# Cross stage of a decoder layer: values by head group, x2 turned behind the values, scores ahead of the slot scores, and the softmax division on VectorE

## The chip, the cores and the metric

One core of one Trainium2 chip. The metric is the device time of one execution in microseconds, as a median of runs. The engines are named as the profile names them: PE is TensorE's matmul, PEld its weight load, DVE VectorE, ACT ScalarE, POOL GpSimd, SP SyncE, which here issues the DMAs.

## The reference, cut to what matters

One decoder layer on x of 2 x 2048 tokens with 512 features, all float32: a Mamba-like mixer, a cross attention on a context of 77 tokens, and a feed-forward part in which 16 slots gather the tokens, 16 experts work on the slots, and the tokens read the slots back. The change touches the cross attention and the gathering of the slots:

```python
    def _L0_xattn_ref(x, context, q_w, q_b, k_w, k_b, v_w, v_b, o_w, o_b):
        ...
        q = (x @ q_w + q_b).reshape(B, T, H, D).transpose(0, 2, 1, 3)
        k = (context @ k_w + k_b).reshape(B, S, H, D).transpose(0, 2, 1, 3)
        v = (context @ v_w + v_b).reshape(B, S, H, D).transpose(0, 2, 1, 3)
        att = jnp.einsum('bhtd,bhsd->bhts', q, k) / jnp.sqrt(jnp.float32(D))
        causal = jnp.tril(jnp.ones((T, S), dtype=bool))
        att = jnp.where(causal[None, None, :, :], att, -jnp.inf)
        att = jax.nn.softmax(att, axis=-1)
        y = jnp.einsum('bhts,bhsd->bhtd', att, v)
        y = y.transpose(0, 2, 1, 3).reshape(B, T, C)
        return y @ o_w + o_b
    ...
    x = _layernorm(x + _L0_attn_ref(...), axis=-1)        # x1
    x = _layernorm(x + _L0_xattn_ref(x, ctx_1024, ...), axis=-1)        # x2
    x = _layernorm(x + _L0_ffn_ref(x, ...), axis=-1)
```

There are 16 heads of 32 features. The feed-forward part begins with an attention of the 16 slots over all tokens of x2, which the kernel computes with a running maximum and a running sum while it makes x2.

## The kernel before

The kernel runs five stages one after the other: tables, mixer, cross, experts, combine, each a block with its own programs for PE, ACT, DVE, POOL and SP, which meet only through semaphores. The cross stage (`cross_stage`) takes the 4096 tokens in 32 tiles of 128, 16 for each of two sequences. For tile t:

- `turn_x1` (PE, L934) turns x1 of the tile, `take_x1T` (ACT, L1017) copies it from PSUM, `queries` (PE, L943) multiplies it with the query weights, `take_queries` (DVE, L1080) adds the bias.
- `score` (PE, L954) makes the scores of the 16 heads with 77 context tokens. `take_scores` (DVE) adds the causal mask in the first tile of a sequence only (L1069), takes the maximum over the context (L1072) and subtracts it (L1074).
- `exponents` (ACT, L1021), `denominators` (DVE, sum L1102, reciprocal L1105), `normalise` (L1138) multiplies the 128 x 1232 exponentials with the reciprocals, in place.
- `turn_probs` (PE, L961) turns the probabilities into the four PSUM banks that held the scores, `take_probsT` (ACT, L1044) copies them out bank by bank, `weigh_values` (PE, L970) multiplies with the values, `take_yT` (ACT, L1060) copies the result, `project_out` (PE, L978) projects.
- `residual` (DVE, L1124) adds x1 plus bias, which `add_bias` (POOL, L1134) has made, and `norm` (DVE, L578 to L595, fifteen small instructions) makes the factors of the layernorm; `scale_rows` (ACT, L1050) writes x2.
- `turn_x2` (PE, L985), `take_x2T` (ACT, L1027), `slot_scores` (PE, L993), `slot_maxima` (DVE, L1089 to L1098), `slot_exponents` (ACT, L1033, L1036), `slot_sums` (DVE, L1110, L1112), `turn_slots` (PE, L1001), `take_slotsT` (ACT, L1055), `weigh_tokens` (PE, L1011) and `add_tokens` (DVE, L1118) carry the tile's x2 into the slots.

The order is written out by hand: each engine has a function `step` for one tile, in which stages of several tiles stand beside each other. The softmax of tile t + 1, the slot scores of tile t - 1 and add_tokens of tile t - 2 run in the step of tile t. `tiles` runs the steps 0 to 3, 14 to 17 and 30 and 31 written out, and 4 to 13 and 18 to 29 in hardware loops of two steps a turn. An engine takes its instructions in order, so one that waits holds up all behind it. `wait_later` leaves a wait out in the first tiles. PSUM: four banks `SC` for scores and turned probabilities, one each for `AV` (queries, then weighed values), `TO` (turned x2, projection, tokens' product), `SLOT` and `TOK` (turned x1, tokens' product). `add_tokens` must have read TOK and TO before x1 or x2 is turned into them.

SP loads x1 two tiles ahead and stores x2 and its transpose. In steps 1, 14 and 16 it fetches the first two, four and six of the 96 weight units of the experts into a ring of six.

The step of PE before:

```python
                def step(t, u, half, seq):
                    turn_probs(pe, t)
                    if before(t, 1):
                        turn_x2(pe, t - 1, 1 - u)
                    if ahead(t, 2):
                        turn_x1(pe, t + 2, u, half + 1)
                    weigh_values(pe, t, seq(0))
```

Of the kernel before, what the change touches and what calls it, by code (L numbers as in the profile page):

```python
# [876 lines left out]
def cross_stage(nc, io, hold, ring, ring_in):  # L877
    with Stage(nc, "crs") as st:
# [34 lines left out]
        HEAD_AT = [(h % HG) * GROUPS + h // HG for h in range(HEADS)]  # L913
# [43 lines left out]
        def turn_probs(pe, t):  # L957
            pe.wait_ge(s["normed"], t + 1)
            for i in range(HG):
                for h in range(GROUPS):  # L960
                    last = nc.tensor.transpose(SC[0:CTX, i, h * P:(h + 1) * P], pr[:, i * GROUPS + h, :], hold["ident"][:])  # L961
                last.then_inc(s["pr_turned"], 1)

        def weigh_values(pe, t, b):
            pe.wait_ge(s["prT_done"], HG * t + HG)

            pe.wait_ge(s["qT_done"], min(t + 2, TILES) if isinstance(t, int) else t + 2)
            for h in range(HEADS):
                g, r = h // HG, (h % HG) * HD
                last = nc.tensor.matmul(AV[r:r + HD, g * P:(g + 1) * P], hold["v"][:, b, h * HD:(h + 1) * HD], prT[:, HEAD_AT[h], :],  # L970
                                        start=True, stop=True)
            last.then_inc(s["av_done"], 1)
# [67 lines left out]
        def take_probsT(act, t):  # L1040
            wait_later(act, s["av_done"], t)
            for i in range(HG):
                act.wait_ge(s["pr_turned"], HG * t + i + 1)
                nc.scalar.activation(prT[:, i * GROUPS:(i + 1) * GROUPS, :].rearrange("p h t -> p (h t)"), SC[0:CTX, i, :], ACT.Copy).then_inc(s["prT_done"], 1)  # L1044
# [91 lines left out]
        def normalise(pool, t):  # L1136
            pool.wait_ge(s["rden_done"], t + 1)
            nc.gpsimd.tensor_tensor(pr[:], pr[:], broadcast(rden[:].unsqueeze(2), [P, HEADS, CTX]), ALU.mult).then_inc(s["normed"], 1)  # L1138
# [24 lines left out]
        with nc.Block() as block:  # L1163
# [26 lines left out]
            def _(pe):  # L1190
# [8 lines left out]
                def step(t, u, half, seq):  # L1199
                    turn_probs(pe, t)  # L1200
                    if before(t, 1):
                        turn_x2(pe, t - 1, 1 - u)
# [3 lines left out]
                    if before(t, 1):  # L1206
                        slot_scores(pe, t - 1, 1 - u)
                    if ahead(t, 1):
                        score(pe, t + 1, seq(1))
                    project_out(pe, t)  # L1210
# [13 lines left out]
            def _(act):  # L1224
# [4 lines left out]
                def step(t, u, half, seq):  # L1229
                    take_probsT(act, t)  # L1230
                    if before(t, 1):
                        take_x2T(act, t - 1, 1 - u, half - 1 + u)
                    if ahead(t, 2):
                        take_x1T(act, t + 2)
                    take_yT(act, t)
                    if before(t, 1):
                        slot_exponents(act, t - 1)
                    if ahead(t, 1):
                        exponents(act, t + 1)
                    if before(t, 1):  # L1240
                        take_slotsT(act, t - 1)
                    scale_rows(act, t, u, half)
# [6 lines left out]
            def _(dve):  # L1249
# [7 lines left out]
                denominators(dve, 0)  # L1257

                def step(t, u, half, seq):
                    if before(t, 2):  # L1260
                        add_tokens(dve, t - 2, seq(-2))
                    if ahead(t, 1):
                        take_queries(dve, t + 1)
                    if before(t, 1):
                        slot_maxima(dve, t - 1, seq(-1))
                    if ahead(t, 1):
                        take_scores(dve, t + 1, isinstance(t, int) and (t + 1) % CHUNKS == 0)
# [3 lines left out]
                    if ahead(t, 1):  # L1271
                        denominators(dve, t + 1)
# [8 lines left out]
            def _(pool):  # L1281
                pool.wait_ge(s["ob_in"], 16)
                add_bias(pool, 0, 0, 0)
                normalise(pool, 0)

                def step(t, u, half, seq):
                    if ahead(t, 1):
                        add_bias(pool, t + 1, 1 - u, half + u)
                        normalise(pool, t + 1)
# [682 lines left out]
```

## Time and profile before

| | us |
|---|---|
| three runs | 1689.98, 1685.02, 1688.82 |
| median | 1688.82 |
| the profiled execution | 1687.88 |
| its span, first to last instruction | 1686.3 |
| busy in the span: PE / DVE / ACT / POOL | 1429.2 / 805.2 / 445.3 / 232.6 |
| mean granted clock of TensorE | 0.937 of full speed |
| normalise on POOL, 32 times | 71.9 (2.248 each), POOL idle 420.0 ahead of it |

The page cuts the span into 40 slices of 42 us. The cross stage covers slices 12 to 25: PE there is busy nine tenths or more of nearly every slice. The experts follow, in which DMA is busy nine tenths or more; the mixer lies ahead of the cross stage and the combine stage at the end.

A row of the timeline reads: start, duration, engine, line, operation, what it writes and reads, the shape of the output and of the input, count; in brackets how long the engine stood idle before and who released it. Rows of the same kind that follow each other are merged into one.

### The profile page before, as it was taken

Reading aid. Unit: us, or ns where it says so; the run is one execution under the profiler, and the core shown is the slowest. Engines: PE = TensorE matmul, PEld = TensorE weight load, DVE = VectorE, ACT = ScalarE, POOL = GpSimd, SP = SyncE. Lnnn points to the kernel's source line nnn. Section 1 sums busy time; section 2 is a strip of 40 time slices with the busy share of each in tenths; the row PEclk is TensorE's granted clock in tenths of the full one; section 3 lists DMA queues with packets and bytes.
Section 4 is the critical chain, followed back from the end, with each engine's and each line's share of the span. In section 5 each row is a group of like instructions: output and inputs, shape, how many; then the busy total and the mean of one; then the engine's idle time right before and its main releaser. Section 6 shows DMA issues by size and latency. Waiting matters only on the chain. (4 is left out here: it accounts for less than half of the span.)

```text
span 1686.3 us, 26525 instructions
## 1 busy us (share of the span) xinstructions
PE 1429.2 (85%) x9904; PEld 890.9 (53%) x9904; DVE 805.2 (48%) x2200; ACT 445.3 (26%) x939; POOL 232.6 (14%) x208
## 2 busy tenths in 40 slices
PE   7999999999769999999999986756666667668996
PEld 2777777777457777777777763211111111115663
DVE  0646666766646767676676764100000000002897
ACT  1533334333114344434434331000000000001333
POOL 0111110011011212121212111000000000001221
PEclk9999999999979999999999997878888988888999
DMA  9342222122115111134111104699999999991563
GB/s 314 123 130 70 83 88 88 62 65 76 63 44 207 39 55 44 50 144 151 47 47 52 41 38 158 242 423 424 426 428 423 427 423 427 424 417 47 176 216 132
DMA packets 78052, 309.18 MB, mean 183 GB/s; under 512 B 9772, under 2 KB 14892, under 8 KB 61593
## 3 DMA queue, kind: packets, MB, share of 16 engines
q1 hardware_dynamic: 76696, 307.91, 47.4%
q8 instruction: 47, 0.77, 0.2%
q0 software_dynamic: 1024, 0.27, 0.1%
q14 instruction: 29, 0.23, 0.0%
q10 hardware_dynamic: 256, 0.00, 0.0%
HBM read 274.33 MB, written 33.82 MB: 183 GB/s over the span
## 5 line engine op out<-in xcount | busy, mean ns | idle before, releaser
L1375 PE MATMUL exp_bank<-all_ring,exp_hm 128*32 128x512 f32 x976 | 155.6, 761 | 116.4 <-DMA all_ring<-in_e_W 67.2
L1411 DVE TENSOR_TENSOR exp_gu<-exp_up,exp_gate 128x512 f32<-128x512 f32 x16 | 11.1, 692 | 418.7 <-ACT exp_gate L1420 418.7
L160 PE MATMUL mix_bank<-all_ring,mxw_win 128*128 128x256 f32 x672 | 157.1, 387 | 3.4 <-POOL all_ring L828 3.4
L1375 PEld LDWEIGHTS exp_bank<-all_ring,exp_hm 128*32 128x32 f32 x976 | 30.8, 125 | 227.4 <-DMA all_ring<-in_e_Wg 80.1
L160 PEld LDWEIGHTS mix_bank<-all_ring,mxw_win 128*128 128x128 f32 x672 | 126.8, 192 | 30.0 <-issue 7.6
L1138 POOL TENSOR_TENSOR crs_pr<-crs_pr,crs_rden 128x1232 f32<-128x1232 f32 x32 | 71.9, 2248 | 420.0 <-DVE crs_rden L1105 420.0
L1397 PE MATMUL exp_bank<-all_ring,exp_guT 128*32 128x512 f32 x512 | 110.5, 666 | 13.7 <-DVE exp_guT L1414 12.6
L943 PE MATMUL crs_bank<-crs_x1T,att_q_w 128*128 128x128 f32 x1024 | 121.3, 277 | 0.7 <-ACT crs_x1T L1017 0.7
L943 PEld LDWEIGHTS crs_bank<-crs_x1T,att_q_w 128*128 128x128 f32 x1024 | 118.5, 194 | 1.6 <-ACT crs_x1T L1017 1.1
L978 PE MATMUL crs_bank<-att_o_w,crs_yT 128*128 128x512 f32 x256 | 118.3, 605 | 0.0
L230 DVE SCALAR_TENSOR_TENSOR all_ring<-all_ring,mxw_taps 128x256 f32<-128x256 f32 x192 | 84.6, 482 | 64.2 <-ACT all_ring L179 61.9
L706 PE MATMUL mix_bank<-mxw_wout,all_ring 128*128 128x512 f32 x256 | 112.7, 593 | 1.6 <-DVE all_ring L756 1.6
L1420 ACT ACTIVATE exp_up<-exp_bank 128x512 f32<-128x512 f32 x16 | 9.6, 597 | 318.5 <-PE exp_bank L1382 318.5
L706 PEld LDWEIGHTS mix_bank<-mxw_wout,all_ring 128*128 128x128 f32 x256 | 48.5, 190 | 56.4 <-issue 53.6
L1089 DVE TENSOR_REDUCE crs_tile_top<-crs_bank 128x2 f32<-128x256 f32 x32 | 13.6, 425 | 130.4 <-PE crs_bank L993 130.4
L961 PEld LDWEIGHTS crs_scores<-all_ident,crs_pr 128*77 128x77 f32 x512 | 59.5, 151 | 26.6 <-POOL crs_pr L1138 19.2
L1397 PEld LDWEIGHTS exp_bank<-all_ring,exp_guT 128*32 128x32 f32 x512 | 27.0, 121 | 85.7 <-issue 65.3
L213 POOL TENSOR_TENSOR all_ring<-all_ring,all_dwv 128x512 f32<-128x512 f32 x24 | 30.8, 1282 | 297.7 <-ACT all_dwv L199 296.4
L978 PEld LDWEIGHTS crs_bank<-att_o_w,crs_yT 128*128 128x128 f32 x256 | 46.0, 189 | 48.3 <-issue 45.9
L961 PE MATMUL crs_scores<-all_ident,crs_pr 128*77 128x128 f32 x512 | 62.9, 277 | 9.9 <-POOL crs_pr L1138 9.9
L1050 ACT ACTIVATE crs_x<-crs_xr,crs_stats 128x512 f32<-128x512 f32 x32 | 26.0, 813 | 158.7 <-DVE crs_stats L595 158.7
L993 PE MATMUL crs_bank<-crs_x2T,att_m 128*128 128x128 f32 x512 | 66.5, 284 | 0.7 <-ACT crs_x2T L1027 0.7
(269 smaller groups left out, 2348.2 us busy)
## 6 DMA issues: line engine op xcount, KB each, us to landing
all_ring<-in_e_W SPq DMA_DIRECT2D x62, 2048.0 KB, 26.0
all_ring<-in_e_Wg SPq DMA_DIRECT2D x31, 2048.0 KB, 27.0
all_ring<-in_xT SPq DMA_DIRECT2D x8, 1024.0 KB, 8.0
all_ring<-scratch_rates SPq DMA_DIRECT2D x64, 128.0 KB, 4.1
all_z<-in_x SPq DMA_DIRECT2D x16, 512.0 KB, 3.9
crs_x<-scratch_x SPq DMA_DIRECT2D x32, 256.0 KB, 2.8
scratch_x<-crs_x SPq DMA_DIRECT2D x32, 256.0 KB, 2.0
scratch_x2T<-crs_x2T SPq DMA_DIRECT2D x32, 256.0 KB, 2.0
```

The lines of the kernel that those rows point to most:

```text
L160: last = nc.tensor.matmul(bank[:, i * BT:(i + 1) * BT], hold["win"][:, k, m * P:(m + 1) * P], hold["xT"][b % 2][:, k, :], start=(k == 0), ...
L213: last = nc.gpsimd.tensor_tensor(conv, conv, product[:, k, :, :], ALU.add)
L230: last = nc.vector.scalar_tensor_tensor(conv[:, m0 + i, :], proj[:, m0 + i, k:k + BT], taps[:, m0 + i, k:k + 1], conv[:, m0 + i, :], ALU.m ...
L706: last = nc.tensor.matmul(OUT[b][:], yT[:, b, g * P:(g + 1) * P], wout[:, g, :], start=(g == 0), stop=(g == GROUPS - 1))
L943: last = nc.tensor.matmul(AV[:, g * P:(g + 1) * P], wq[:, k, g * P:(g + 1) * P], x1T[:, k, :], start=(k == 0), stop=(k == KC - 1))
L961: last = nc.tensor.transpose(SC[0:CTX, i, h * P:(h + 1) * P], pr[:, i * GROUPS + h, :], hold["ident"][:])
L978: last = nc.tensor.matmul(TO[:], yT[:, k, :], wo[:, k, :], start=(k == 0), stop=(k == KC - 1))
L993: last = nc.tensor.matmul(SLOT[:, m * P:(m + 1) * P], hold["m1"][:, k, m * P:(m + 1) * P], x2T[u][:, k, :], start=(k == 0), stop=(k == KC ...
L1050: nc.scalar.activation(x2[u][:], xr[:], ACT.Identity, bias=stats[:, 0, 11:12], scale=stats[:, 0, 9:10]).then_inc(s["x2_done"], 1)
L1138: nc.gpsimd.tensor_tensor(pr[:], pr[:], broadcast(rden[:].unsqueeze(2), [P, HEADS, CTX]), ALU.mult).then_inc(s["normed"], 1)
L1375: last = nc.tensor.matmul(bank[w][q * ROWS:(q + 1) * ROWS, :], hm[u][:, k, :], weights[:, at:at + FQ], start=(k == 0), stop=False)
L1397: last = nc.tensor.matmul(bank[3][q * ROWS:(q + 1) * ROWS, :], guT[:, i, q * ROWS:(q + 1) * ROWS], weights[:, (j * 4 + i) * D:(j * 4 + i + ...
```

## The change

It does four things, all in the cross stage.

- `turn_probs` fills the four banks by group of four neighbouring heads, `take_probsT` copies a group at a time, and `weigh_values` waits for each group and not for all four. The number of instructions stays.
- On PE, `turn_x2` moves from behind `turn_probs` to behind `weigh_values`, and `score` moves ahead of `slot_scores`. ACT and DVE take their work in the matching order.
- `normalise` moves from POOL to DVE, directly behind `denominators`.
- On DVE, `denominators` and `normalise` of the next tile stand ahead of `slot_sums` and `residual`, where `denominators` stood behind `residual`; `slot_maxima` moves behind `take_scores`.

```diff
--- before.py
+++ after.py
@@ -910,7 +910,6 @@
                     "slot_turned", "sp_prT_done", "z_done", "z_added")
         x1_in, x2_stored, x2T_stored = st.pair("x1_in"), st.pair("x2_stored"), st.pair("x2T_stored")
         LAST = TILES - 1
-        HEAD_AT = [(h % HG) * GROUPS + h // HG for h in range(HEADS)]
 
         def load(sp, t, u):
             wait_later(sp, s["mix_turned"], t - 1)
@@ -956,19 +955,19 @@
 
         def turn_probs(pe, t):
             pe.wait_ge(s["normed"], t + 1)
-            for i in range(HG):
-                for h in range(GROUPS):
-                    last = nc.tensor.transpose(SC[0:CTX, i, h * P:(h + 1) * P], pr[:, i * GROUPS + h, :], hold["ident"][:])
+            for g in range(GROUPS):
+                for h in range(HG):
+                    last = nc.tensor.transpose(SC[0:CTX, g, h * P:(h + 1) * P], pr[:, h * GROUPS + g, :], hold["ident"][:])
                 last.then_inc(s["pr_turned"], 1)
 
         def weigh_values(pe, t, b):
-            pe.wait_ge(s["prT_done"], HG * t + HG)
-
             pe.wait_ge(s["qT_done"], min(t + 2, TILES) if isinstance(t, int) else t + 2)
-            for h in range(HEADS):
-                g, r = h // HG, (h % HG) * HD
-                last = nc.tensor.matmul(AV[r:r + HD, g * P:(g + 1) * P], hold["v"][:, b, h * HD:(h + 1) * HD], prT[:, HEAD_AT[h], :],
-                                        start=True, stop=True)
+            for g in range(GROUPS):
+                pe.wait_ge(s["prT_done"], GROUPS * t + g + 1)
+                for i in range(HG):
+                    h, r = g * HG + i, i * HD
+                    last = nc.tensor.matmul(AV[r:r + HD, g * P:(g + 1) * P], hold["v"][:, b, h * HD:(h + 1) * HD], prT[:, h, :],
+                                            start=True, stop=True)
             last.then_inc(s["av_done"], 1)
 
         def project_out(pe, t):
@@ -1039,9 +1038,9 @@
 
         def take_probsT(act, t):
             wait_later(act, s["av_done"], t)
-            for i in range(HG):
-                act.wait_ge(s["pr_turned"], HG * t + i + 1)
-                nc.scalar.activation(prT[:, i * GROUPS:(i + 1) * GROUPS, :].rearrange("p h t -> p (h t)"), SC[0:CTX, i, :], ACT.Copy).then_inc(s["prT_done"], 1)
+            for g in range(GROUPS):
+                act.wait_ge(s["pr_turned"], GROUPS * t + g + 1)
+                nc.scalar.activation(prT[:, g * HG:(g + 1) * HG, :].rearrange("p h t -> p (h t)"), SC[0:CTX, g, :], ACT.Copy).then_inc(s["prT_done"], 1)
 
         def scale_rows(act, t, u, half):
             act.wait_ge(s["stats_done"], t + 1)
@@ -1133,9 +1132,9 @@
             wait_later(pool, s["res_done"], t - 1)
             nc.gpsimd.tensor_tensor(x1b[u][:], x1[u][:], ob[:], ALU.add).then_inc(s["x1b_done"], 1)
 
-        def normalise(pool, t):
-            pool.wait_ge(s["rden_done"], t + 1)
-            nc.gpsimd.tensor_tensor(pr[:], pr[:], broadcast(rden[:].unsqueeze(2), [P, HEADS, CTX]), ALU.mult).then_inc(s["normed"], 1)
+        def normalise(dve, t):
+            dve.wait_ge(s["rden_done"], t + 1)
+            nc.vector.tensor_tensor(pr[:], pr[:], broadcast(rden[:].unsqueeze(2), [P, HEADS, CTX]), ALU.mult).then_inc(s["normed"], 1)
 
         def tiles(eng, body):
 
@@ -1198,15 +1197,15 @@
 
                 def step(t, u, half, seq):
                     turn_probs(pe, t)
-                    if before(t, 1):
-                        turn_x2(pe, t - 1, 1 - u)
                     if ahead(t, 2):
                         turn_x1(pe, t + 2, u, half + 1)
                     weigh_values(pe, t, seq(0))
                     if before(t, 1):
-                        slot_scores(pe, t - 1, 1 - u)
+                        turn_x2(pe, t - 1, 1 - u)
                     if ahead(t, 1):
                         score(pe, t + 1, seq(1))
+                    if before(t, 1):
+                        slot_scores(pe, t - 1, 1 - u)
                     project_out(pe, t)
                     if before(t, 1):
                         turn_slots(pe, t - 1)
@@ -1228,16 +1227,15 @@
 
                 def step(t, u, half, seq):
                     take_probsT(act, t)
-                    if before(t, 1):
-                        take_x2T(act, t - 1, 1 - u, half - 1 + u)
                     if ahead(t, 2):
                         take_x1T(act, t + 2)
                     take_yT(act, t)
                     if before(t, 1):
-                        slot_exponents(act, t - 1)
+                        take_x2T(act, t - 1, 1 - u, half - 1 + u)
                     if ahead(t, 1):
                         exponents(act, t + 1)
                     if before(t, 1):
+                        slot_exponents(act, t - 1)
                         take_slotsT(act, t - 1)
                     scale_rows(act, t, u, half)
                 tiles(act, step)
@@ -1255,21 +1253,23 @@
                 take_queries(dve, 0)
                 take_scores(dve, 0, True)
                 denominators(dve, 0)
+                normalise(dve, 0)
 
                 def step(t, u, half, seq):
                     if before(t, 2):
                         add_tokens(dve, t - 2, seq(-2))
                     if ahead(t, 1):
                         take_queries(dve, t + 1)
+                    if ahead(t, 1):
+                        take_scores(dve, t + 1, isinstance(t, int) and (t + 1) % CHUNKS == 0)
                     if before(t, 1):
                         slot_maxima(dve, t - 1, seq(-1))
                     if ahead(t, 1):
-                        take_scores(dve, t + 1, isinstance(t, int) and (t + 1) % CHUNKS == 0)
+                        denominators(dve, t + 1)
+                        normalise(dve, t + 1)
                     if before(t, 1):
                         slot_sums(dve, t - 1, seq(-1))
                     residual(dve, t, u)
-                    if ahead(t, 1):
-                        denominators(dve, t + 1)
                     norm(dve, t)
                 tiles(dve, step)
                 add_tokens(dve, LAST - 1, 1)
@@ -1281,12 +1281,10 @@
             def _(pool):
                 pool.wait_ge(s["ob_in"], 16)
                 add_bias(pool, 0, 0, 0)
-                normalise(pool, 0)
 
                 def step(t, u, half, seq):
                     if ahead(t, 1):
                         add_bias(pool, t + 1, 1 - u, half + u)
-                        normalise(pool, t + 1)
                 tiles(pool, step)
```

## Rows read from the trace of the kernel before

**Rows 1.** Busy time by windows, cross stage and experts; columns on the header line.

```profile
core 0: us, PE busy (x) PEld busy (x) DVE busy (x) ACT busy (x) POOL busy (x), PEclk, DMA share, GB/s
500.00:1000.00 500.00, 481.11 (x4492) 366.75 (x4491) 346.11 (x901) 201.21 (x450) 104.10 (x60) 1.00 0.21 76
1060.00:1440.00 380.00, 254.40 (x1512) 63.55 (x1504) 23.18 (x52) 15.52 (x26) 13.37 (x26) 0.85 0.98 410
```

**Rows 2.** Timeline, 529 to 546 us: the chain of one tile.

```profile
529.21 1.44 DVE L1072 TENSOR_REDUCE crs_top<-crs_scores 128x16 f32<-128x1232 f32 x1
530.69 1.44 DVE L1074 TENSOR_TENSOR crs_pr<-crs_scores,crs_top 128x1232 f32<-128x1232 f32 x1
...
532.16 1.23 ACT L1021 ACTIVATE crs_pr<-crs_pr 128x1232 f32<-128x1232 f32 x1 [2.13 <-DVE crs_pr L1074]
...
533.43 1.44 DVE L1102 TENSOR_REDUCE crs_den<-crs_pr 128x16 f32<-128x1232 f32 x1
534.90 0.25 DVE L1105 RECIPROCAL crs_rden<-crs_den 128x16 f32<-128x16 f32 x1
535.07 0.63 DVE L578 BATCH_NORM_STATS2 crs_stats<-crs_xr 128x6 f32<-128x512 f32 x1
...
538.32 0.21 DVE L595 TENSOR_SCALAR crs_stats<-crs_stats 128x1 f32<-128x1 f32 x1
...
538.57 0.81 ACT L1050 ACTIVATE crs_x<-crs_xr,crs_stats 128x512 f32<-128x512 f32 x1 [4.90 <-DVE crs_stats L595]
539.29 2.02 ACT L1044 ACTIVATE crs_prT<-crs_scores 77x512 f32<-77x512 f32 x4
...
541.37 1.08 PE L970 MATMUL crs_bank<-crs_prT,att_v 77*32 77x128 f32 x32 [0.31 <-ACT crs_prT L1044]
...
542.38 2.05 PE L993 MATMUL crs_bank<-crs_x2T,att_m 128*128 128x128 f32 x16
...
544.36 1.13 PE L954 MATMUL crs_scores<-att_k,crs_qT 32*128 32x77 f32 x32
...
545.66 1.44 DVE L1072 TENSOR_REDUCE crs_top<-crs_scores 128x16 f32<-128x1232 f32 x1
```

**Rows 3.** Timeline, 521 to 541 us: work that lies beside that chain.

```profile
521.14 0.15 PEld L961 LDWEIGHTS crs_scores<-all_ident,crs_pr 128*77 128x77 f32 x1 [0.24 <-POOL crs_pr L1138]
...
532.04 0.15 DVE L1110 TENSOR_TENSOR all_sum<-all_sum,crs_alpha 128x2 f32<-128x2 f32 x1
...
532.71 0.69 DVE L1124 TENSOR_TENSOR crs_xr<-crs_bank,crs_x1b 128x512 f32<-128x512 f32 x1 [0.32 <-PE crs_bank L978]
...
535.23 2.25 POOL L1138 TENSOR_TENSOR crs_pr<-crs_pr,crs_rden 128x1232 f32<-128x1232 f32 x1 [12.98 <-DVE crs_rden L1105]
...
538.02 1.91 PE L961 MATMUL crs_scores<-all_ident,crs_pr 128*77 128x128 f32 x16
...
540.00 0.63 PE L985 MATMUL crs_bank<-all_ident,crs_x 128*128 128x128 f32 x4
540.46 0.60 PE L934 MATMUL crs_bank<-all_ident,crs_x 128*128 128x128 f32 x4
```

**Rows 4.** Timeline of DVE, tile 16, the first of the second sequence.

```profile
744.94 1.44 DVE L1069 TENSOR_TENSOR crs_pr<-crs_scores,att_mask 128x1232 f32<-128x1232 f32 x1
...
762.85 1.44 DVE L1072 TENSOR_REDUCE crs_top<-crs_scores 128x16 f32<-128x1232 f32 x1
```

**Rows 5.** Timeline, 612 to 629 us, a tile in the first hardware loop.

```profile
612.13 1.44 DVE L1072 TENSOR_REDUCE crs_top<-crs_scores 128x16 f32<-128x1232 f32 x1
...
621.24 0.21 DVE L595 TENSOR_SCALAR crs_stats<-crs_stats 128x1 f32<-128x1 f32 x1
...
621.76 1.41 DVE L1118 SCALAR_TENSOR_TENSOR all_z<-all_z,crs_alpha,crs_bank 128x512 f32<-128x512 f32 x2 [0.30 <-issue]
...
624.37 1.08 PE L970 MATMUL crs_bank<-crs_prT,att_v 77*32 77x128 f32 x32
...
628.77 1.44 DVE L1072 TENSOR_REDUCE crs_top<-crs_scores 128x16 f32<-128x1232 f32 x1
```

## Prediction

> **What bounds the kernel now.** I read the utilisation by windows first, then the timeline of one tile, then the same places in other tiles. The change touches only the cross stage, 32 tiles between 480 and 1031 us. In its steady part TensorE is busy for 481 of 500 us at the full granted clock, VectorE for 346 [rows 1]; that invites the reading "TensorE bounds it". The timeline shows otherwise. I follow two moments: S, where DVE starts the scores' maximum (L1072), and X, where DVE ends the layernorm (L595). For tiles 3 and 2, S is 529.21 [rows 2]. From there one step hands to the next: subtraction 530.69, exponential on ACT 532.16, sum 533.43, reciprocal 534.90, layernorm 535.07 to X = 538.53. Then ACT writes x2 (L1050, 538.57) and, behind it in its own order, copies the turned probabilities (L1044, 539.29 to 541.31); PE weighs values at 541.37, does the slot scores at 542.38 and the scores at 544.36; the next S is 545.66 [rows 2]. So the loop closes: S to X 9.32, X to S 7.13, period 16.45, with no slack in it. PE stands idle in this tile 0.31 us before the values [rows 2] and about 0.07 before it turns x2 (turned probabilities end 539.93, next start 540.00) [rows 3]: its own demand is 16.45 - 0.38 = 16.07 us.
>
> Tile 16 tests this. It has one more DVE step, the mask (L1069, 1.44 us), and there S to S is 762.85 - 744.94 = 17.91 [rows 4], 1.46 more than 16.45. A DVE step put into this loop is paid in full. In the tiles inside the hardware loops (4 to 13 and 18 to 29) the period is 16.64 (628.77 - 612.13) [rows 5].
>
> After the cross stage the experts run from DRAM: DMA share 0.98 between 1060 and 1440 [rows 1]. Only 6 of their 96 weight units are loaded ahead, and they stay 6, so the stream starts when the cross stage ends; I take a shift of that end one to one into the total.
>
> **The change part by part, for a tile outside the loops.**
>
> S to X, on DVE. The sum and reciprocal are unchanged: reciprocal at S + 5.69 [rows 2]. The new multiplication has no row on DVE, but the subtraction L1074 and the masking L1069 have its form, 128x1232 from 128x1232 with a second operand, at 1.44 [rows 2, 4]. It needs the reciprocal: 0.25 + 0.03 (the gap between sum and reciprocal, 533.43 + 1.44 to 534.90), so it runs S + 5.97 to S + 7.41. The bounds of this price are 1.44 and POOL's 2.25 for the same work [rows 3]; I take 1.44, the same engine's. Next come the slot sums. Today they lie under the exponential (532.04, 0.15 each) [rows 3]; now they cost about 0.25. The residual L1124 (0.69) also lies under it today (532.71) [rows 3]; now it starts at about S + 7.62 and ends at S + 8.31. Under the exponential there now stands the slot maximum, which used to stand ahead of S: neutral. The layernorm starts at S + 8.34 and lasts 538.53 - 535.07 = 3.46 [rows 2]. X = S + 11.80, against 9.32: **+2.48**.
>
> X to S, on ACT and PE. L1050 and the four copies are not touched: the last copy ends where it did, and the values' last group may start at X + 2.84 (541.37 - 538.53). Values by group: three of four groups can now run before, which hides 3/4 of 1.01 (541.37 to 542.38) = 0.76. The slot scores leave the path: 1.98 (542.38 to 544.36) [rows 2]. Turning x2 enters it: 0.46 (540.00 to 540.46) [rows 3]. The scores to S stay 1.30 (544.36 to 545.66) [rows 2]. So X to S = 2.84 + 0.25 + 0.46 + 1.30 = 4.85, against 7.13: **-2.28**. Period 16.65: **+0.20**.
>
> Moving POOL's multiplication away saves nothing on its own: it ends at 537.48 and PE, still busy with the tokens' product, starts the turned probabilities at 538.02 [rows 3]. PE will now reach them near S + 10.8 and has them done by S + 12.7; the x1 turn then waits for add_tokens on DVE, as the x2 turn does today, and PE idles there about half a microsecond instead of before the values. POOL's add_bias runs earlier; nobody waits for it. The four waits in front of the value groups can cost something each. The trace has no such wait; below zero is excluded, since the copies set the earliest start; above, I take 0.24, the gap that PEld shows before this chain's turned probabilities [rows 3], once per tile on the path (the last group). SP's queue: the store of x2T and the load behind it go out some 1.5 us later in a period of 16, and the load's tile is needed a period later: nothing. ACT: the copy of x2T now comes after yT; it ends near X + 4.5, and the slot scores need it at about X + 4.6, with a microsecond to spare before DVE wants their result.
>
> **In the hardware loops** every second tile has a jump back on DVE: X is 621.45, but add_tokens starts at 621.76 with 0.30 of "issue" and ends at 623.17, X + 1.72 [rows 5]. Today that ties with the copies (values at 624.37, X + 2.92). In the new order it is followed by the x1 turn and the four value groups: x1 at X + 1.77, the queries' bias done near X + 2.3, values from X + 2.40, all 1.01 of them, x2 0.47, scores 1.30: X to S 5.18 against 7.32, so 11.80 + 5.18 = 16.98, +0.34. The other tile: values at X + 2.99 today (ACT starts 0.16 later than outside), so 5.00, period 16.80, +0.16. Mean of the pair +0.25.
>
> **Sum.** S is followed from tile 2 to tile 31, 29 periods: 20 in the loops at 0.25 = 5.0, 9 others at 0.20 = 1.8. The last S to X gives +2.48 with no gain behind it. In the last tile the slot scores wait for x2T and push the output projection by about 0.9 (an estimate from the parts above). At the start the first multiplication ends 0.87 earlier (1.44 + 0.03 against 2.25 + 0.09) and the first value groups give 0.76: about -1.5. Total 5.0 + 1.8 + 2.5 + 0.9 - 1.5 = **+8.7 us**. The profiled execution took 1687.88 us (span 1686.3), 0.9 under the median of 1688.82; I add the sum to the median: **1697.5 us**, +0.5%.
>
> **Rivals.**
> 1. *PE's floor, faster.* If PE's own work bounds the stage, removing its idle time is all that counts, and the shorter way from X to S gives just that: the mean period falls from 16.6 to about 16.1, 29 x 0.5 = 14.5, with the start 16: 1673 us. For it: the 481 busy of 500 [rows 1]. Against it: tile 16. It decides where DVE's additions fall under 2.28, and is full under about 1.7, that is with a multiplication of 0.7 instead of 1.44. The Trainium skill ("GPSIMD Engine Reference", section "Elementwise — side-by-side cycle accounting") gives GPSIMD 1.96 times DVE's time for tensor_tensor and tells to use DVE for elementwise work; it would expect this change to gain. What its advice leaves out is where the work stands: here 0.54 us lie between POOL's end and PE's start [rows 3]. Against a fast multiplication it speaks itself: "VectorE: DVE Perf Modes" (section "Why `tensor_tensor` can't do 2×_2P or 4×") says that a two-tensor operation gets no second element per cycle in fp32.
> 2. *The two shifts cancel, same.* My +2.48 and -2.28 differ by less than a fifth of a microsecond; ACT's late start of 0.16 in the loops could vanish now that PE and DVE reach their waits in another order. Then the loops give +0.05 on average: 1.0 + 1.8 + 1.9 (end less start) = +4.7 at most, 1688 to 1693.5.
> 3. *Waits by group cost, slower than forecast.* 0.24 per tile over 31 tiles is 7.4 us: 1705 us. In the jump-back tiles all the groups lie on the path.
>
> **How the numbers follow.** Forecast (1694 to 1701) 0.45; rival 3, 0.2; rival 2, 0.2; rival 1, 0.15. The range for 8 in 10 takes in rivals 2 and 3: 1688 to 1706. 0.3% of 1688.8 is 5.1 us, about what a measurement can tell from no change. Slower (over 1693.9) 0.66, same 0.19, faster (under 1683.8) 0.15.
>
> **What would show it.** In the profile after: L1138 on DVE at 1.44; S to X near 11.8; the residual straight after the slot sums with no wait; X to S near 4.9 outside the loops and 5.0 and 5.2 inside; PE idle moved to the x1 turn, released by add_tokens, 0.5 or more; period 16.65 outside, 16.9 inside; the experts' stage as long as before. A period near 16.1, or PE waits that do not name DVE, would prove me wrong; so would X to S well over 5.2, with gaps between the value groups.

## The result: 1.5% slower, three times the forecast difference

The changed kernel takes 1715.00 us (median of six runs, 1709.08 to 1717.61) against 1688.84 (six runs, 1684.76 to 1693.36): ratio 1.015, interval 1.0125 to 1.0176, **+26 us** where +8.7 was forecast. The sign is right; the time lies above the range (1688 to 1706). The profiled execution took 1710.22 us, span 1708.6, so 22.3 of the 26 us can be looked for in the trace.

The head of the page after, and then the two windows of [rows 1]:

```profile
span 1708.6 us, 26558 instructions
...
PE 1433.4 (84%) x9904; PEld 890.3 (52%) x9904; DVE 853.4 (50%) x2232; ACT 448.5 (26%) x939; POOL 162.1 (9%) x176
```

```profile
500.00:1000.00 500.00, 467.97 (x4332) 350.31 (x4332) 377.37 (x897) 197.47 (x435) 36.74 (x29) 0.99 0.21 75
1060.00:1440.00 380.00, 248.32 (x1490) 64.06 (x1493) 30.18 (x78) 14.93 (x25) 13.80 (x27) 0.87 0.97 406
```

The work is the same (PE 1433.4 us against 1429.2), but PE is busy for 468 of the 500 us in place of 481, and DVE for 377 in place of 346. New idle time of PE: who ends it, in the list of waits of PE from 480 to 1060 us (total, times, longest):

```profile
PE crs_bank L933 <- DVE all_z L1117: 20.9, 22, 1.3
...
PE crs_bank L969 <- ACT crs_prT L1043: 5.3, 2, 3.2
...
PE crs_bank L933 <- DMA crs_x<-scratch_x: 3.2, 2, 1.7
```

PE waits for `add_tokens` on DVE in front of the x1 turn, in 22 of 32 tiles, 0.95 us on average: a loop over DVE, ACT and PE bounds the stage, and it is now longer. The last line is new too; it matters below. The tile of [rows 2], on DVE, ACT, PE and PEld (timeline, lines of the changed kernel are one lower):

```profile
528.76 1.44 DVE L1071 TENSOR_REDUCE crs_top<-crs_scores 128x16 f32<-128x1232 f32 x1 [3.06 <-PE crs_scores L953]
...
530.51 3.60 PE L977 MATMUL crs_bank<-att_o_w,crs_yT 128*128 128x512 f32 x8
...
532.97 1.44 DVE L1101 TENSOR_REDUCE crs_den<-crs_pr 128x16 f32<-128x1232 f32 x1
534.44 0.25 DVE L1104 RECIPROCAL crs_rden<-crs_den 128x16 f32<-128x16 f32 x1
534.73 1.44 DVE L1137 TENSOR_TENSOR crs_pr<-crs_pr,crs_rden 128x1232 f32<-128x1232 f32 x1
536.09 0.15 DVE L1109 TENSOR_TENSOR all_sum<-all_sum,crs_alpha 128x2 f32<-128x2 f32 x1
...
536.38 0.69 DVE L1123 TENSOR_TENSOR crs_xr<-crs_bank,crs_x1b 128x512 f32<-128x512 f32 x1
537.11 0.69 DVE L578 BATCH_NORM_STATS2 crs_stats<-crs_xr 128x6 f32<-128x512 f32 x1
...
540.42 0.21 DVE L595 TENSOR_SCALAR crs_stats<-crs_stats 128x1 f32<-128x1 f32 x1
540.55 1.40 DVE L1117 SCALAR_TENSOR_TENSOR all_z<-all_z,crs_alpha,crs_bank 128x512 f32<-128x512 f32 x2
...
541.39 2.02 ACT L1043 ACTIVATE crs_prT<-crs_scores 77x512 f32<-77x512 f32 x4
...
542.05 0.63 PE L933 MATMUL crs_bank<-all_ident,crs_x 128*128 128x128 f32 x4 [0.68 <-issue]
542.61 1.28 PE L969 MATMUL crs_bank<-crs_prT,att_v 77*32 77x128 f32 x32
...
543.46 0.16 PEld L969 LDWEIGHTS crs_bank<-crs_prT,att_v 77*32 77x32 f32 x8 [0.26 <-ACT crs_prT L1043]
...
543.82 0.65 PE L984 MATMUL crs_bank<-all_ident,crs_x 128*128 128x128 f32 x4
544.40 1.13 PE L953 MATMUL crs_scores<-att_k,crs_qT 32*128 32x77 f32 x32
...
545.60 1.44 DVE L1071 TENSOR_REDUCE crs_top<-crs_scores 128x16 f32<-128x1232 f32 x1 [3.06 <-PE crs_scores L953]
```

S to X is 540.63 - 528.76 = 11.87 (forecast 11.80), X to S 4.97 (4.85), the period 16.84 (16.65). The last of the four value groups is held by ACT's last copy (0.26 on PEld); the x2 turn stands 0.36 behind that group's start, and the scores 0.58 behind the x2 turn. The x1 turn starts 0.10 behind the end of `add_tokens` (540.55 + 1.40), although this row labels its 0.68 us of idle time "issue".

| | before | after | shift | forecast |
|---|---|---|---|---|
| S of tile 2 | 512.76 | 511.35 | -1.4 | -1.5 |
| 29 periods to S of tile 31 | 482.70 | 498.75 | +16.05 | +6.8 |
| S of tile 31 to the next X | | | +2.55 | +2.5 |
| last X to the end of tile 31's layernorm | 13.61 | 15.93 | +2.3 | +0.9 |
| experts' first step | 1033.36 | 1053.03 | +19.7 | +8.7 |
| from there to the end | 652.9 | 655.6 | +2.7 | 0 |

In the twelve other kernels of this study the last line was 651.4 to 658.4, without a pattern: I count it as spread of executions. Most of the miss sits in the periods.

The first line agrees with its forecast by luck. The cross stage itself began earlier in this execution: S of tile 0 is 479.42 against 481.65, and in `f2_after_early` and `f3_after_filler`, which have the same instructions up to there, it is 478.73 and 481.23. From S of tile 0 to S of tile 2 the changed kernel takes 31.93 us against 31.11: 0.8 less in step 0 and 1.6 more in step 1, where TensorE's clock fell (shown below). So the start cost 0.8 where the forecast had it give 1.5.

### The profile page after: what moved, and what is told of

It reads as the page before. It is cut to its first block and busy times, and to the rows that moved or that the text cites. A ratio compares the mean times of both kernels' runs of the same rounds, so it can differ in the third digit from the quotient of the medians.

```text
span 1708.6 us, 26558 instructions
## 1 busy us (share of the span) xinstructions
PE 1433.4 (84%) x9904; PEld 890.3 (52%) x9904; DVE 853.4 (50%) x2232; ACT 448.5 (26%) x939; POOL 162.1 (9%) x176
## 5 line engine op out<-in xcount | busy, mean ns | idle before, releaser
L1373 PE MATMUL exp_bank<-all_ring,exp_hm 128*32 128x512 f32 x976 | 151.9, 745 | 119.0 <-DMA all_ring<-in_e_W 67.5
L1133 POOL TENSOR_TENSOR crs_x1b<-crs_x,crs_ob 128x512 f32<-128x512 f32 x32 | 40.5, 1267 | 570.3 <-DVE crs_xr L1123 491.7
L1071 DVE TENSOR_REDUCE crs_top<-crs_scores 128x16 f32<-128x1232 f32 x30 | 43.2, 1441 | 100.8 <-PE crs_scores L953 100.8
L992 PE MATMUL crs_bank<-crs_x2T,att_m 128*128 128x128 f32 x512 | 70.3, 294 | 1.4 <-ACT crs_x2T L1026 1.4
L1020 ACT ACTIVATE crs_pr<-crs_pr 128x1232 f32<-128x1232 f32 x32 | 39.3, 1230 | 115.0 <-DVE crs_pr L1073 115.0
```

Of the source, the lines that this page charges most:

```text
L992: last = nc.tensor.matmul(SLOT[:, m * P:(m + 1) * P], hold["m1"][:, k, m * P:(m + 1) * P], x2T[u][:, k, :], start=(k == 0), stop=(k == KC ...
L1020: nc.scalar.activation(pr[:], pr[:], ACT.Exp, scale=SCALE).then_inc(s["exp_done"], 1)
L1071: nc.vector.tensor_reduce(top[:].rearrange("p (i h) -> p i h", i=HG), src, AX.X, ALU.max).then_inc(s["top_done"], 1)
L1133: nc.gpsimd.tensor_tensor(x1b[u][:], x1[u][:], ob[:], ALU.add).then_inc(s["x1b_done"], 1)
L1373: last = nc.tensor.matmul(bank[w][q * ROWS:(q + 1) * ROWS, :], hm[u][:, k, :], weights[:, at:at + FQ], start=(k == 0), stop=False)
```

## The experiments

A ratio is to the kernel before, run on the same chip with each group of kernels.

### The division alone, in both orders

`e1_pool_div`: the changed kernel with the division back on POOL.

```diff
-        def normalise(dve, t):
-            dve.wait_ge(s["rden_done"], t + 1)
-            nc.vector.tensor_tensor(pr[:], ...)
+        def normalise(pool, t):
+            pool.wait_ge(s["rden_done"], t + 1)
+            nc.gpsimd.tensor_tensor(pr[:], ...)
```

> The changed kernel with the division back on POOL; everything else stays. Theory (the loop over DVE sets the period; the division on DVE is its added step): the multiplication's 1.47 us leave S to X, which falls from 11.87 to about 10.3; with X to S at 5.0 the loop would close in 15.3, under PE's own demand of 16.1 to 16.3, so that PE becomes the bound: period about 16.3, time 1674 to 1686 us, faster than before. Rival (the new order on PE is what costs, by its turn-arounds and its later x1 turn): the period stays at 16.8 or more outside the loops and the time over 1700.

Measured: 1674.59 us, ratio 0.9923 (0.9906 to 0.994). The period is 15.77 in every undisturbed tile, S to X 10.35. By windows (PE, PEld, DVE, ACT, POOL busy, granted clock):

```profile
600.00:640.00 40.00, 40.00 (x410) 31.10 (x409) 27.72 (x73) 18.07 (x38) 8.27 (x6) 1.00 0.15 52
```

PE has no idle time left: here TensorE is the bound. With the division as the only difference the changed kernel is 1.015 / 0.9923 = 2.3% slower, some 40 us. On DVE the division adds 1.52 us to S to X (11.87 against 10.35); on POOL its 2.25 us keep PE waiting in 3 tiles only. PE's bound takes a part of that back: without the division the loop would close in 10.35 + 4.97 = 15.32, but PE needs 15.77. So the period differs by 1.07 outside the loops and 1.40 inside (17.17 on average): 9 x 1.07 + 20 x 1.40 = 38 us.

Even here S to X is 1.03 longer than the 9.32 of the kernel before. That is the new order, not the division: the projection now stands behind the slot scores and ends 5.35 us behind S in the changed kernel (530.51 + 3.60), where it ended 3.46 behind it. DVE is at the sum by then, so the residual and the slot sums can't lie under the exponential any more. The prediction had this term right.

`e2_before_dve_div`: the kernel before with the division on DVE, behind `denominators` and ahead of `norm`.

```diff
                     if ahead(t, 1):
                         denominators(dve, t + 1)
+                        normalise(dve, t + 1)
                     norm(dve, t)
```

> The kernel before with the division on DVE behind the denominators, nothing else. Theory: S to X grows by the multiplication's 1.47 us and nothing takes it back: period 17.9 instead of 16.45 outside the loops, 31 x 1.47 = 45 us, time 1734. Rival (POOL's slow multiplication was on the path too, so that 0.8 us come back per tile): 1710.

Measured: 1772.4 us (two runs), ratio 1.0507 (1.048 to 1.0534), nearly 40 us more than expected. S to X grew by 1.52 where 1.47 was expected, and some periods were 17.97 and 18.16; others were 19.6 to 21.3. PE in one of those, and two windows:

```profile
619.96 0.66 PE L985 MATMUL crs_bank<-all_ident,crs_x 128*128 128x128 f32 x4 [1.61 <-DVE all_z L1118]
...
621.57 1.92 PE L970 MATMUL crs_bank<-crs_prT,att_v 77*32 77x128 f32 x32 [0.53 <-ACT crs_prT L1044]
623.42 3.78 PE L993 MATMUL crs_bank<-crs_x2T,att_m 128*128 128x128 f32 x16
```

```profile
603.00:615.00 12.00, 11.98 (x126) 9.30 (x125) 7.86 (x14) 4.24 (x11) 1.27 (x1) 1.00 0.13 45
620.00:632.00 12.00, 11.47 (x96) 8.86 (x97) 4.56 (x10) 3.99 (x13) 0.00 (x0) 0.72 0.19 66
```

After PE stood idle for 1.61 and 0.53 us the slot scores take 3.78 us in place of 2.05 [rows 2], and the granted clock of the stretch is 0.72: TensorE ran part of it at its lower level, 1.2 GHz. New idle time of PE was paid twice, once as a wait and once in the clock. `h1_dve_filler` tests that: the same kernel with twelve transposes per tile, which nobody reads, where PE stands idle.

```diff
                     turn_probs(pe, t)
+                    wait_later(pe, s["slot_exp"], t - 1)
+                    for _ in range(12):
+                        nc.tensor.transpose(SLOT[:, 0:P], hold["ident"][:], hold["ident"][:])
```

> The kernel before with the division on DVE, and on PE 12 transposes of the identity matrix that nobody reads between the turned probabilities and the x2 turn of every tile (1.3 us of the 1.6 to 2.0 us that PE stands idle there). They add no result. Without them this kernel took 1772 us, with tiles of 17.97 to 18.2 us and others of 19.6 to 21.3 in which PE ran at the lower clock. Theory (the added DVE step costs 1.47 us a tile, the rest is the clock that falls in PE's idle time): all tiles take 18.0 to 18.2 and the time is 1730 to 1740 us. Rival (the long tiles come from something else): 1765 to 1780.

Measured: 1736.61, ratio 1.0288 (1.0267 to 1.031). All tiles but the first and the one with the mask take 17.97 to 18.17, and

```profile
500.00:1000.00 500.00, 477.61 (x4437) 373.35 (x4435) 359.10 (x857) 183.90 (x410) 35.63 (x28) 1.00 0.20 72
```

the clock is 1.00 where `e2_before_dve_div` had 0.92. With PE given work for nothing, the kernel is 36 us faster. So the division on DVE in the order before costs 2.9% directly (31 x 1.52 = 47 us) and another 2.2% by the clock.

### Values by group

`e4_before_groups`: the kernel before with the groups only; `turn_probs`, `take_probsT` and `weigh_values` as in the diff of the change, all else untouched.

```diff
-            pe.wait_ge(s["prT_done"], HG * t + HG)
+            for g in range(GROUPS):
+                pe.wait_ge(s["prT_done"], GROUPS * t + g + 1)
```

> The kernel before with the values by group alone; order and division as before. Theory: the values end at X + 3.5, bound by add_tokens, the two turns and four groups on PE, and no longer at X + 3.84: 0.34 us less in tiles without a jump back on DVE, nothing in the others: about 20 x 0.34 = 7 us less than before, 1682. Rival (waits between groups break up PE's stream): no gain or a loss.

Measured: 1679.59, ratio 0.9962 (0.9948 to 0.9977). The period is 16.07 outside the loops (16.45 before), and inside 16.11 and, where DVE jumps back, 16.50 to 16.57 (16.64 before).

`e3_pool_nogroups` is `e1_pool_div` with one wait for all four copies; `h2_after_nogroups` is the changed kernel with the same edit.

```diff
+            pe.wait_ge(s["prT_done"], GROUPS * t + GROUPS)
             for g in range(GROUPS):
-                pe.wait_ge(s["prT_done"], GROUPS * t + g + 1)
```

> As the first kernel (division on POOL, new order), but the values wait once for all four copies. Theory: PE is the bound there and arrives at the values about when the last copy ends, so one wait costs 0 to 0.2 us a tile: 0 to 6 us more than the first kernel. Rival (the four waits between the value groups cost PE more than they hide): it is faster than the first kernel.

> The changed kernel with one wait for all four copies in front of the values. Theory (the loop over DVE is the bound, so what stands between the last copy and the scores counts in full): the values' first three groups, 0.65 to 0.76 us, come back onto the way from X to S outside the loops and in the tiles without a jump back, about 0.4 us in the others; 16 to 20 us more than the changed kernel, 1733 us, and more if PE's longer idle time lets its clock fall. Rival (the grouping saves nothing here because add_tokens and the x1 turn are what the values wait for): 1715.

Measured: 1695.67, ratio 1.0063 (1.004 to 1.0085), 21 us over `e1_pool_div` where 0 to 6 were expected; and 1749.12, ratio 1.0359 (1.0338 to 1.0381), 34 over the changed kernel, where 16 to 20 were expected. The waits of PE, in `e3_pool_nogroups`:

```profile
PE crs_bank L969 <- ACT crs_prT L1043: 16.9, 29, 3.0
```

and in `h2_after_nogroups`:

```profile
PE crs_bank L969 <- ACT crs_prT L1043: 23.8, 30, 4.6
```

The values wait for the last copy in nearly every tile. I had taken this as covered with the division on POOL; it isn't, since PE has no slack there (period 16.23 against 15.77: 29 x 0.46 = 13; for the rest see `f4_nogroups_early`). In `h2_after_nogroups` the tiles outside the loops that nothing else disturbs take 17.60 against 16.84, and those in the loops 17.68 to 17.77 against 17.17: 9 x 0.76 + 20 x 0.55 = 18, as expected. But most of its tiles take 18.2 to 19.2, and the mean clock over 500 to 1000 us is 0.93: the other half of the 34 us is the clock. The groups are worth 7 us in the order before and 21 and 34 in the new one. In the order before, two turns stand ahead of the values, so they can start only 0.38 us earlier than with one wait (16.45 to 16.07); in the new order only one does. Rival 3 (each group's wait costs) falls: the groups gain in all three, and where the copies are in already, as in `e1_pool_div`, the values with four waits take 1.08 us, as they do before with one [rows 2].

### x2 turned behind the values

`h3_after_x2_first`: the changed kernel, with x2 turned directly behind the probabilities again (PE), and copied there (ACT). Groups, scores first and the division on DVE stay.

```diff
                     turn_probs(pe, t)
+                    if before(t, 1):
+                        turn_x2(pe, t - 1, 1 - u)
                     if ahead(t, 2):
                         turn_x1(pe, t + 2, u, half + 1)
                     weigh_values(pe, t, seq(0))
-                    if before(t, 1):
-                        turn_x2(pe, t - 1, 1 - u)
```

> The changed kernel with the x2 turn back behind the turned probabilities, on PE and ACT alike; scores stay ahead of the slot scores, values by group, division on DVE. Theory (the x2 turn costs 0.58 us behind the values, where it is on the loop): x2 at X + 1.46, x1 at X + 1.92, values X + 2.5 to 3.5, scores to S 1.25: X to S 4.75 against 4.97, in the jump-back tiles 5.3 against 5.35; 0.1 to 0.2 us a tile, 3 to 6 us less than the changed kernel: 1710 us. Rival (turning x2 ahead of x1 delays the values by as much as it saves): no difference to the changed kernel, 1715.

Measured: 1695.99 us (nine runs), ratio 1.0037 (1.0024 to 1.005), **19 us under the changed kernel** (14.7 between the profiled executions) where 5 were expected. PE in the same tile:

```profile
540.78 0.63 PE L984 MATMUL crs_bank<-all_ident,crs_x 128*128 128x128 f32 x4 [0.73 <-DVE all_z L1117]
541.25 0.60 PE L933 MATMUL crs_bank<-all_ident,crs_x 128*128 128x128 f32 x4
541.78 1.08 PE L969 MATMUL crs_bank<-crs_prT,att_v 77*32 77x128 f32 x32
542.79 1.13 PE L953 MATMUL crs_scores<-att_k,crs_qT 32*128 32x77 f32 x32
```

Two turns stand ahead of the values, so the last copy is in when its group comes: the values take 1.08 in one piece and not 1.28, and the scores follow 1.01 behind their start. X to S is 4.67 outside the loops against 4.97, of which the gap ahead of the last group is 0.20 and the turn between values and scores the rest; the periods are 16.54, and 16.57 and 16.99 in the loops (16.84, 17.10 and 17.25 after). No wait for a DMA is left either. The experts start 15.1 us earlier in its profile (1037.9 against 1053.0): 20 x 0.39 + 9 x 0.30 = 10.5 from the periods, 1.5 from the DMA waits, the rest at the two ends of the stage.

### The DMA queue, and the clock at the stage's start

In the changed kernel, and in no tile of the one before, PE waits for a load of x1, 1.70 us in step 17. PE there, and SP's queue ahead of it:

```profile
783.96 0.66 PE L933 MATMUL crs_bank<-all_ident,crs_x 128*128 128x128 f32 x4 [1.70 <-DMA crs_x<-scratch_x]
```

```profile
769.18 0.33 SPq L925 DMA_DIRECT2D scratch_x2T<-crs_x2T  x1
769.56 1.04 SPq L870 DMA_DIRECT2D all_ring<-in_e_W  x2
770.70 0.41 SPq L917 DMA_DIRECT2D crs_x<-scratch_x  x1
```

In both kernels the fetch of 4 MB of weights goes out directly ahead of x1's 256 KB. But the store of x2T, ahead of both, now waits for a later copy: this load of x1 was issued 2.38 us ahead of S of tile 17 before (760.47) and is issued 1.05 behind it now. x1 lands some 13 us after its issue, just ahead of the turn at 783.96. `f1_pool_early` (on `e1_pool_div`), `f2_after_early` (on the changed kernel) and `f4_nogroups_early` (on `e3_pool_nogroups`) issue the fetch ahead of the stores:

```diff
                         load(sp, t + 2, u)
+                    if isinstance(t, int) and t in FIRST_UNITS:
+                        for unit in FIRST_UNITS[t]:
+                            prefetch(sp, io, ring, ring_in, 0, unit)
```

> Division on POOL, new order, values by group, and in SP's step the experts' first weight units are fetched right behind the load of x1, ahead of the two stores of x2, and no longer behind them. Theory (in steps 14 and 16 the next load of x1 stands behind 4 MB of weights, and in the new order it is issued later because the store of x2T is; PE then waits for it at the x1 turn, 1.5 us twice, and those tiles took 18.96 and 17.53 us where their neighbours take 15.77): both waits vanish, the tile with the mask comes to about 17, the other to 15.8, 3 to 4 us less than the kernel with the fetch as it was: 1671 us. Rival (the weights fetched earlier collide with the load of their own step): new waits for x1 in steps 1, 14 or 16, no gain.

> The changed kernel with that one edit to SP's step. Theory: its two waits of PE for x1 (1.5 and 1.7 us, tiles of 18.96 and 17.70 us) vanish and these tiles come to 18.3 and 16.85, 1.5 us less than the changed kernel in all, 1713 us by its median: the late load is a small part of what the prediction missed. Rival (it set off more than its two tiles): 1708 or less.

> Division on POOL, new order, one wait for all four copies, and the early fetch. The kernel without the early fetch lost 3.7 us in the mask tile (20.14 where 16.24 and the mask's 1.46 make 17.7 at most), 0.9 and 1.5 in the two after it. Theory (the wait of 1.7 us for x1 let PE's clock fall as well): with the wait gone the clock stays up and 4 to 6 us come back: 1690 us. Rival (the clock falls there by the mask tile's own longer idle time): 2 us or less.

Measured: 1670.45, ratio 0.9895 (0.9867 to 0.9924), 4 us under `e1_pool_div`; the intervals of the two overlap, but its two tiles take 17.25 and 15.76 in place of 18.96 and 17.53; 1713.96, ratio 1.0165 (1.014 to 1.019), tiles 18.31 and 16.85 in place of 18.96 and 17.70, so 1.5 us, which the medians can't tell; and 1688.85, ratio 1.0008 (0.9992 to 1.0023), 7 under `e3_pool_nogroups`. In `e3_pool_nogroups` the wait for x1 (1.67 us) was followed by slot scores of 3.78 us, so the wait had cost the clock too. The wait for the DMA is gone in each.

`f3_after_filler` keeps PE busy in steps 1 and 31 of the changed kernel:

```diff
+                    if isinstance(t, int) and t in (1, LAST):
+                        wait_later(pe, s["slot_exp"], t - 1)
+                        for _ in range(24 if t == 1 else 16):
+                            nc.tensor.transpose(SLOT[:, 0:P], hold["ident"][:], hold["ident"][:])
                     weigh_values(pe, t, seq(0))
```

> The changed kernel with transposes of the identity matrix that nobody reads on PE ahead of the values, 24 in step 1 and 16 in step 31, where PE stands idle 3.2 and 2.1 us. They add no result. Theory (after those idle stretches PE's granted clock falls to the lower of its two levels, and the values, x2 turn, scores and slot scores behind them take up to twice their time): the clock stays at the upper level, step 1 closes in 16.4 where it took 18.04, the next in 16.85 where it took 17.41, and the last step gains 1.4: 3 to 3.5 us less than the changed kernel, 1711.5 us. Rival (these tiles are slow for another reason): the same times with full-speed PE instructions, or the filler itself delays the values.

In the changed kernel PE stands idle for 3.17 us in step 1, and between 506 and 512 us its clock is 0.65:

```profile
506.36 1.94 PE L969 MATMUL crs_bank<-crs_prT,att_v 77*32 77x128 f32 x32 [3.17 <-ACT crs_prT L1043]
...
511.21 3.68 PE L992 MATMUL crs_bank<-crs_x2T,att_m 128*128 128x128 f32 x16
```

```profile
506.00:512.00 6.00, 5.53 (x71) 3.96 (x72) 0.65 (x1) 3.33 (x7) 0.00 (x0) 0.65 0.39 126
```

With the filler:

```profile
506.00:512.00 6.00, 5.34 (x87) 3.91 (x86) 1.56 (x5) 4.38 (x8) 0.00 (x0) 1.00 0.11 44
```

Its slot scores take 2.05, and step 1 takes 16.55 in place of 18.04. In step 31 the slot scores take 2.05 as well, in place of 3.66. Yet the median is 1715.3, ratio 1.0169 (1.0152 to 1.0186): no gain. Step 2 took 17.56 (expected 16.85), since PE, earlier now, ran into a late load of x1, behind the two weight units of step 1:

```profile
525.85 0.66 PE L933 MATMUL crs_bank<-all_ident,crs_x 128*128 128x128 f32 x4 [1.57 <-DMA crs_x<-scratch_x]
```

Step 30 took 17.83 in place of 16.93. And in its profiled execution the clock fell elsewhere, in tiles of 18.70 and 17.81 between 740 and 820 us (0.96 over that stretch). That PE, idle for about a microsecond in each tile, loses its clock now and then, would also explain why the changed kernel's median lies 4.8 us above its profiled run. The mean granted clocks of its six runs fit that: 0.941 in the two of 1709.08 and 1710.22 us, 0.931 to 0.935 in the four of 1714.04 to 1717.61. Where in those four it fell no trace shows, and this part stays open.

### A version that beats both

`g1_best` is `f1_pool_early` with 8 and 16 unread transposes in steps 1 and 31:

```diff
+                        for _ in range(8 if t == 1 else 16):
```

> The fastest so far (division on POOL, new order, values by group, early fetch; 1670.5 us) with 8 unread transposes in step 1 and 16 in step 31 ahead of the values. Theory (PE's clock falls after the idle time there and makes step 1 take 16.8 us): step 1 closes in 16.0 and the last step is shorter by up to 1.4; 1 to 2 us less, 1669 us, which is at the edge of what can be told. Rival: no gain.

Measured: 1664.32 (five runs, 1661.16 to 1665.92), ratio **0.9852** (0.9834 to 0.987), 1.5% faster than the kernel before. It is the change without its move of the division, with the fetch earlier and the unread transposes. Steps 1 and 2 take 15.01 and 15.77, where they took 15.56 and 16.82 in `f1_pool_early`; the 16.8 that the expectation names for step 1 is step 2's. No run combines this with x2 turned ahead of x1.

## Why the prediction was wrong in size

**What held.** That the loop of DVE, ACT and PE bounds the stage, and not PE's 481 of 500; that an added DVE step is paid in full; the multiplication at 1.44, and its chain: S to X 11.87 against 11.80. That PE's idle time moves to the x1 turn behind `add_tokens`. The last S to X, +2.55. Rival 1 didn't come true, and `e1_pool_div` puts a number on it: with POOL's slower multiplication the kernel takes 2.3% less. The Trainium skill's advice for DVE ("GPSIMD Engine Reference", "Elementwise — side-by-side cycle accounting") stood beside that rival; it gives a ratio of 1.96 between the two engines, and the rows here give 2.25 / 1.44 = 1.56. "VectorE: DVE Perf Modes" ("Why `tensor_tensor` can't do 2×_2P or 4×") of the Trainium skill agrees with the row: 1.44 us, as the subtraction of the same size.

**X to S was summed from durations that the new neighbours don't keep.** The step "2.84 + 0.25 + 0.46 + 1.30" was 4.97 outside the loops, not 4.85. The last group starts where I put it (X + 2.83), but needs 0.36 until the x2 turn starts, not a quarter of 1.01; from that turn to the scores it is 0.58, not the 0.46 that separates it from another turn [rows 3]; from the scores to S it is 1.20, not 1.30: the slot maxima no longer stand in front of S. With 0.07 more from S to X (0.06 of it in the layernorm, 3.52 against 3.46) the period grows by 0.40, not 0.20. In the loops the jump-back tile came to 5.35 (forecast 5.18) and the other to 5.23 (5.00), by the same two gaps around the x2 turn for the most part, so the period grows by 0.53 and not 0.25. The mechanism was right and the terms around the x2 turn were too small: `h3_after_x2_first`, which takes that turn out again, comes back to 4.67. The sum was a difference of two terms of 2.3 to 2.5, and an error of 0.1 to 0.2 in either doubles it. Over 29 tiles: 20 x 0.53 + 9 x 0.40 = 14.2 in place of 6.8. The range held the prices of waits, but not this.

**"SP's queue: nothing" failed.** I looked at when the load's tile is needed, not at what stands ahead of it in the queue once the store of x2T is late: in steps 14 and 16, 4 MB of weights. Two tiles are 1.5 us longer by it.

**The clock was left out.** The forecast moved idle time of PE without asking what PE's clock does behind it. Step 1 and the step after took 18.04 and 17.41. In step 31, where PE stood idle for 2.10 and, behind the x2 turn, for 0.69 us, the slot scores took 3.66 us:

```profile
1026.50 3.66 PE L992 MATMUL crs_bank<-crs_x2T,att_m 128*128 128x128 f32 x16 [0.69 <-ACT crs_x2T L1026]
```

The granted clock from 1026.5 to 1030 is 0.52. (The values ahead of them take 1.78, but at a clock of 1.00: they wait for each copy.) That is most of the last step's +2.3 (forecast 0.9), 0.6 of the periods, and 1.5 in step 1, ahead of S of tile 2. For the periods: 14.2 + 1.5 + 0.6 = 16.3, against 16.05 counted.

**PE's own demand isn't period less idle.** I had 16.45 - 0.38 = 16.07; with PE as the bound it is 15.77. The difference of 0.30 can be read from start to start, in the tile of [rows 2] and in the same tile of `e1_pool_div`. The values start 0.91 behind the x1 turn there and 0.53 here, 0.38 more where I counted 0.31 as idle; the turn behind the turned probabilities starts 1.98 behind them there and 1.75 here, 0.23 more where I counted 0.07. So 0.23 of the 0.30 is waiting that the trace, whose ends of matmuls are modelled, shows as busy. The rest depends on neighbours: slot scores 1.98 against 1.89 and the projection 3.53 against 3.44, less the x2 turn's 0.58 against 0.46. The changed kernel's period lies 1.07 above the floor of 15.77.

**The parts, as the runs price them.** Division on DVE, about +40 us in the new order. Values by group, -34 in the changed kernel. x2 behind the values, +19. These prices hold in their surroundings and don't add up; scores ahead of the slot scores, with DVE's new order, was not run by itself. Without the division the change gains 0.8%, with the fetch moved 1.05%.

## What to carry to other kernels

Where a cyclic chain over several engines sets the period, an operation is priced by whether it stands on the chain, not by its engine's rate: 2.25 us on an idle engine beside the chain beat 1.44 us on it by 2.3% of the kernel's time. When a forecast is a small difference of two large shifts, price each new pair of neighbours by its own row; where there is no such row, widen the range by the uncertainty of each gap times the number of tiles. Whenever an edit leaves TensorE idle, ask about the clock behind the gap. And ask of a queue whose instructions are unchanged which of its transfers now goes out later, and what stands behind it. Last, a forecast line that agrees can agree by luck: the start of the stage did.

## What the runs showed of the hardware that I had not expected

- PE idle for 1.6 us and then 0.5 us was followed by slot scores of 3.78 us, where the same sixteen matmuls take 2.05, while unread transposes in the gap kept the granted clock at 1.00: 1736.61 against 1772.4 us.
- The scores start 0.58 us behind the start of an x2 turn (`e1_pool_div` and the changed kernel); an x1 turn starts 0.46 behind an x2 turn [rows 3], and the values 0.53 behind an x1 turn in `e1_pool_div`.
- A 256 KB load issued behind 4 MB of weights took about 13 us (changed kernel, step 17); the median of its kind is 2.7.
